# Cross-attention and feed-forward on one core: loads of CT and VQ and stores of VS issued by ScalarE, values taken one batch per step

## What is computed

```python
q = fq_sym((layernorm(x) @ Wq + bq) * scale, axis=-1)      # per row and head
k, v = split(cond @ Wkv + bkv)
k = fq_sym(k, axis=-1)
v = fq_sym(v, axis=2)                                       # one scale per column, over all keys
attn = fq_unsigned(softmax(q @ k.T), axis=-1)
x = x + (attn @ v) @ Wp + bp
xq = quant_input(layernorm(x)); x1, x3 = split(xq @ w13.T)
x = x + quant_input(rmsnorm(relu(x1)**2 * x3) * norm_w) @ w2.T
```

## Time and profile before

| | |
|---|---|
| Median of 3 runs | 1955.6 us |
| Profiled execution | 1956.41 us, its span 1954.5 us |
| TensorE | 85% busy, granted clock 0.90 of 2.4 GHz on average |
| VectorE | 87% busy |
| ScalarE | 70% busy |
| GpSimd | 74% busy |
| DMA queue of SyncE | packets take 80.3% of 16 engines' span, 325.38 MB |
| The loop's exps | from 186.6 to 1685.8 us |

### The profile page before, as it was taken

The page is one execution under the profiler, slowest core; times in us unless marked ns, Lnnn a source line. Parts: engine busy times, 40 slices in busy tenths (PEclk is TensorE's granted clock), DMA queues, the critical chain, the costliest instruction groups (busy, mean ns, idle before and its releaser), DMA issues.

```text
span 1954.5 us, 40604 instructions
## 1 busy us (share of the span) xinstructions
PE 1665.0 (85%) x16216; PEld 1134.0 (58%) x16216; DVE 1693.2 (87%) x2665; ACT 1372.1 (70%) x1324; POOL 1444.0 (74%) x1166
## 2 busy tenths in 40 slices
PE   7997888888788888887888888878988888579997
PEld 6884666665555666555566564434445555368875
DVE  6766999999879999997999999989999999776663
ACT  2445988898688888886888888777778778532221
POOL 1341788998898888988898899988997888623222
PEclk9998999998989999987999997556688998789999
DMA  5676989998989899999999998997988987642221
GB/s 166 220 204 164 197 192 196 181 202 183 211 167 205 181 199 184 188 199 195 193 189 186 203 177 167 198 165 135 184 161 157 207 168 144 129 111 45 63 55 44
DMA packets 862283, 327.97 MB, mean 168 GB/s; under 512 B 786128, under 2 KB 815888, under 8 KB 862096
## 3 DMA queue, kind: packets, MB, share of 16 engines
q1 hardware_dynamic: 862096, 325.38, 80.3%
HBM read 83.30 MB, written 48.63 MB: 67 GB/s over the span
## 4 chain that ended last, share of the span: by engine, by line
DVE 38%; PE 25%; issue 14%; POOL 11%; DMA 6%; ACT 5%; SPq 2%; POOLq 0%; DVEq 0%; ACTq 0%
DVE S L1141 34%; POOL PT L1384 7%; PE PS L660 5%; PE PS L764 5%; DMA PP<-Pr 3%; PE PK L815 3%; PE PK L600 3%; PE PS L627 2%; ACT Pr L967 2%; PE PK L602 2%; PE PO L679 2%; POOL VQ L1319 1%; PE PO L600 1%; PE PO L602 1%; SPq L544 1%
## 5 line engine op out<-in xcount | busy, mean ns | idle before, releaser
L1141 DVE TENSOR_SCALAR_CACHE_REDUCE S<-PS,SQN 128x1536 f32<-128x1536 f32 (+1 forms) x768 | 1287.0, 1714 | 92.0 <-PE PS L660 73.6
L967 ACT ACTIVATE Pr<-S,MS 128x5888 uint8<-128x5888 f32 x200 | 1041.4, 5207 | 234.7 <-DVE MJ L1163 157.2
L1384 POOL CAST PT<-PP 128x1536 uint16<-128x1536 uint8 (+1 forms) x800 | 1097.5, 1417 | 90.7 <-DMA PP<-Pr 89.3
L660 PE MATMUL PS<-KT,QT 96*128 96x512 bf16 (+1 forms) x2496 | 717.5, 413 | 132.8 <-DVE S L1141 121.6
L679 PEld LDWEIGHTS PO<-VI,PT 128*128 128x128 f16 x9200 | 349.4, 99 | 327.6 <-issue 144.1
L679 PE MATMUL PO<-VI,PT 128*128 128x32 bf16 x9200 | 365.9, 180 | 91.9 <-ACT AO L925 66.0
L660 PEld LDWEIGHTS PS<-KT,QT 96*128 96x128 bf16 (+1 forms) x2496 | 210.0, 105 | 343.1 <-issue 164.6
L600 PE MATMUL PK<-WG,CT 128*128 128x128 f32 (+1 forms) x1272 | 223.7, 306 | 14.1 <-DMA CT<-ctxt 9.5
L602 PE MATMUL PK<-CT,WG 128*128 128x128 f32 (+1 forms) x1272 | 212.0, 294 | 0.0
L600 PEld LDWEIGHTS PK<-WG,CT 128*128 128x128 f32 (+1 forms) x1272 | 175.6, 202 | 17.3 <-issue 13.2
L602 PEld LDWEIGHTS PK<-CT,WG 128*128 128x128 f32 x1272 | 166.3, 193 | 1.4
(11 more groups left out here) (154 smaller groups left out, 1456.0 us busy)
## 6 DMA issues: line engine op xcount, KB each, us to landing
CT<-ctxt SPq DMA_DIRECT2D x180, 256.0 KB, 3.3
k_rows<-KS SPq DMA_DIRECT2D x44, 512.0 KB, 4.1
v_rows<-VS SPq DMA_DIRECT2D x33, 256.0 KB, 4.0
VQ<-v_rows SPq DMA_DIRECT2D x33, 256.0 KB, 3.8
q_rows<-QS SPq DMA_DIRECT2D x13, 512.0 KB, 4.1
W13F<-w13T SPq DMA_DIRECT2D x16, 352.0 KB, 4.1
PP<-Pr SPq DMA_TRANSPOSE x200, 6.1
XT<-x SPq DMA_DIRECT2D x12, 256.0 KB, 3.3
```

What stands on the lines that cost most here:

```text
L660: last = pe.matmul(PS[n % 2][p0:p0 + r, f:f + w], QT[h % 3][0:PARTS * HD, q0:q0 + r], KT[h % 3][0:PARTS * HD, c * CHUNK + f:c * CHUNK + f ...
L967: act.activation(Pr[i % 2].rearrange("p t q b -> p t b q"), S[i % 2].rearrange("p (t b q) -> p t b q", b=2, q=P), ACT.Exp, bias=MS[:, i % ...
L1141: v.tensor_scalar(S[i % 2][:, c * CHUNK:c * CHUNK + CW[c]], PS[n % 2][:, 0:CW[c]], neg_step, None, ALU.mult, ALU.min, accum_out=MN[:, i % ...
L1384: gp.tensor_copy(PT[i % 2][:, 2 * t0:2 * t1, :].rearrange("p (t b) q -> p t b q", b=2), PP[i % 2][:, t0:t1, :].bitcast(U8).rearrange("p t ...
```

## The change

ScalarE gets `load_unit`, `store_v` and `load_v` and issues them in its step right behind exp(i); inside the loop SyncE no longer issues them (ahead of the loop it still loads CT). The waits ahead of each DMA are the same and move with it. The transposes stay on SyncE. The values are taken over twelve steps: one load of VQ per step, `v_quant` due at the last unit's step + 4.95 + b, and `turn_v`, which follows `v_loads`, one per step.

```diff
             for b in range(NBT):
-                v_loads.setdefault(STEP_OF_UNIT[g, NU - 1] + 4 + b // 2, []).append((g, b))
+                v_loads.setdefault(STEP_OF_UNIT[g, NU - 1] + 4 + b, []).append((g, b))
...
         @block.sync
...
                     if u == 0:
                         load_wg(g)
-                    load_unit(g, u)
-                for g, b in dve_batches.get(i, []):
-                    store_v(g, b)
                 for g, b in dve_batches.get(i - K_STORE, []):
                     store_k(g, b)
-                for g, b in v_loads.get(i, []):
-                    load_v(g, b)
...
         @block.scalar
...
+            def load_unit(g, u):
+                k = g * NU + u
+                n = unit_rows(u)
+                act.wait_ge(M["s_ku"], k - RING + 1)
+                act.dma_start(CT[k % RING][:, :, 0:n], ctxl if u == NU - 1 else ctxt[u]).then_inc(s_ct[k % RING], 16)
+
+            def store_v(g, b):
+                kb, us = g * NBT + b, BATCH[b]
+                act.wait_ge(M["s_kve"], g * NU + us[-1] + 1)
+                act.dma_start(Vd[g - 1, :, us[0] * P:(us[-1] + 1) * P],
+                              VS[kb % 2][:, 0:len(us) * P]).then_inc(M[f"s_vd{kb % 2}"], 16)
+
+            def load_v(g, b):
+                kb, us = g * NBT + b, BATCH[b]
+                act.wait_ge(M[f"s_vd{kb % 2}"], 16 * stored_v(kb))
+                if kb >= NBT + 3:
+                    act.wait_ge(M["s_vg"], kb - NBT - 2)
+                act.dma_start(VQ[kb % 3][:, 0:len(us) * P],
+                              Vd[g - 1, :, us[0] * P:(us[-1] + 1) * P]).then_inc(s_vq[kb % 3], 16)
...
                                scale=-1.0, accum_out=ZB[:, i:i + 1]).then_inc(M["s_exp"], 1)
+                for g, u in UNITS.get(i + 3, []):
+                    load_unit(g, u)
+                for g, b in dve_batches.get(i, []):
+                    store_v(g, b)
+                for g, b in v_loads.get(i, []):
+                    load_v(g, b)
                 for g, b in dve_batches.get(i - K_SPLIT, []):
                     k_high(g, b)
...
         @block.gpsimd
...
-                             (end + 4.95 + b // 2, v_quant, (g, b))]
+                             (end + 4.95 + b, v_quant, (g, b))]
```

More of the change, by code:

```diff
@@ L331, in load_unit @@
                 sp.dma_start(CT[k % RING][:, :, 0:n], ctxl if u == NU - 1 else ctxt[u]).then_inc(s_ct[k % RING], 16)
-            def store_v(g, b):
-                kb, us = g * NBT + b, BATCH[b]
-                sp.wait_ge(M["s_kve"], g * NU + us[-1] + 1)
-                sp.dma_start(Vd[g - 1, :, us[0] * P:(us[-1] + 1) * P],
-                             VS[kb % 2][:, 0:len(us) * P]).then_inc(M[f"s_vd{kb % 2}"], 16)
             def store_k(g, b):
@@ L355, in load_wg @@
                 sp.dma_start(WG[:, :, 1, :], wkv_v[:, :, C + g * GC:C + (g + 1) * GC]).then_inc(M["s_wg1"], 16)
-            def load_v(g, b):
-                kb, us = g * NBT + b, BATCH[b]
-                sp.wait_ge(M[f"s_vd{kb % 2}"], 16 * stored_v(kb))
-                if kb >= NBT + 3:
-                    sp.wait_ge(M["s_vg"], kb - NBT - 2)
-                sp.dma_start(VQ[kb % 3][:, 0:len(us) * P],
-                             Vd[g - 1, :, us[0] * P:(us[-1] + 1) * P]).then_inc(s_vq[kb % 3], 16)
             def turn_v(g, b):
```

## The result

After: 1980.28 us (median of 6 runs, 1972.48 to 1997.42), against 1960.07 us of the kernel before in the same runs (1954.83 to 1965.29): ratio 1.0115, interval [1.0083, 1.0148]. The forecast was 1937 us, faster. The kernel is 1.15% slower, and the time lies outside the predicted range of 1920 to 1978. The profiled execution took 1980.81 us, its span 1979.0, with a granted clock of 0.887 on average.

The account below looks back on a forecast made before the run. No engine is full; most of the loop runs at VectorE's pace, with 40.0 us lost to a ring where values are taken. 1956.4 - 40.0 + 14 + 0 + 5 + 2 = 1937.4, forecast 1937 us, range 1920 to 1978.

Parts of the forecast that it names:

- Two queues: DMA engines: PP, no longer in line with CT, may land later by what a CT takes; 5 us, bounds 0 and 15.
- The rule set against this step: DMAs of several engines share 16 DMA engines, only issue time is saved; read so that VQ lands no sooner, 1953.
- The value stretches: Three twelve-step stretches taking values of groups 1 to 3: 40.0 us lost, 14 to stay; some 94, 92 and 86 us.
- Exp's wait for PP: Sign of being right: exp's waits for the transpose of the probabilities under 35 us in all instead of 77.1.
- GpSimd was to wait under 8 us for VQ: Sign of being right: GpSimd's waits for the loads of VQ, 20.5 us before, under 8 us.
- the sign that bunching was not the cause: Sign of being wrong: the three stretches where values are taken stay over 97 us.
- The issues: Loads of CT, stores and loads, 105 us of issues, move to ScalarE's queue and lie under exp's 5.21 us; 0.
- The hold of ScalarE behind a PP issue: In the slower rival: one hold behind a 4.06 us PP issue in each of 36 store steps, up to 146 us.
- Later values: Group 1's last transposes of VB land 2.3 to 3.6 us late for TensorE once; some 2 us at VectorE.
- The rival that was slower: ScalarE pays for issues between exp and the next unit's evacuation: 36 us over 36 store steps, 1973; chance 0.17.
- the small terms: Terms beside the value stretches: issues 0, two queues 5, later values 2 us; their bounds give the likeliest case's range.
- The range: Likeliest case's own range 1922 to 1946 us; with the rivals 1920 to 1978, some 2 in 10 left out.

Follow-up runs that it names:

- all three with pairs: Changed kernel with the old schedule: loads of CT and VQ and stores of VS on ScalarE, values two batches per step; 1.0214 against the kernel before, 1998.03 us.
- the good version: Kernel before with values one batch per step and each load of VQ issued a step earlier, all DMAs on SyncE; 0.9878, 1934.91 us.
- the quarter loads: Kernel before with CT's loop loads issued by ScalarE, only 32 of 128 partitions loaded; 0.9940, against 0.9953 with the same cut loads on SyncE.

## Why the prediction was wrong

**"Two queues" is the step that failed.** It was put at 5 us, with bounds 0 and 15, because a PP "may land later by what a CT takes" and ScalarE had 0.9 us a step to spare. The runs give 20 us for the loads of CT, 21 us for the stores of VS and nothing clear for the loads of VQ; all three with pairs cost 2.1%. Two things were missed. First, how long a PP is delayed, and how many are: 108 of the 200 have an issue of ScalarE that starts inside their own, and land in 8.0 us instead of the 6.6 of the same steps before, the worst in 13.5. No row of the kernel before could give that, since it has no second issuer. Second, the slack was read off the wrong engine. ScalarE had room on average, but PP's ring runs over SyncE and GpSimd, which in the same neighbours had 78.4 of 88.9 and 76.2 of 87.0 us busy and a transpose to wait for. The page already showed exp waiting 77.1 us for PP, 34 times, and GpSimd 89.3 us: that was the tile whose landing to price.

The rule set against this step, that DMAs of several engines share 16 DMA engines and only issue time is saved (the Trainium skill, "DMA: Bandwidth & Descriptors", Issuing engines are not separate DMA queues), points the right way, and these runs go further: here the second issuer did harm. As predicted against that rule, VQ did come in time when issued from ScalarE (waits of 6.3 instead of 32.7 us at the same schedule), and a load placed one step earlier on SyncE did it at no cost.

**The value stretches: right in direction, too much by 8 us.** 26 of 40 us were to come back, 18.4 did. The stretches were to be 94, 92 and 86 us, which is 28 us less and not the sum's 26; they were 100.0, 97.7 and 84.2. With only the values' DMAs on ScalarE 22.8 came back, and 29 with the early loads on SyncE, so 11 left where 14 were taken. The 4.4 us between 22.8 and 18.4 go with the loads of CT, the one difference between those two kernels. Exp's wait for PP was to fall under 35 us. It rose to 99.7; in the good version it is 36.9. GpSimd was to wait under 8 us for VQ, and waited 17.0. Two of the three stretches stayed over 97 us, which was to be the sign that bunching was not the cause. As a sign it misleads: spreading together with early loading brings these two to 93.1 and 93.8.

**The issues: right.** They were put at 0, since ScalarE's queue runs ahead of exp. Of the 131 loads of CT, 102 start within 0.1 us of their exp, 23 up to 2 us ahead of it and none more than 0.5 us behind. They take 0.34 us in the median, and the quarter loads, as many, cost nothing that can be told apart. The cover's worth was shown as well: ahead of exp the same issues cost 20 us more. The hold of ScalarE behind a PP issue that was feared (146 us) did not come; with a PP issue of 6.38 us running, CT's took 0.36.

**Later values: low.** 2 us were taken for step 54; VectorE waits 4.6 us there in the kernel after and 7.3 in the good version. TensorE waits for the last VI there (3.9 and 6.2 us), as was argued.

**The rival that was slower** had the sign, and its 1973 us lay nearest to the 1980, by luck: its mechanism, ScalarE paying for the issues, was not the one. The harm done to a transpose by a copy from elsewhere was given as a small term of the forecast and not as a rival.

**The range.** Its lower end of 1922 is the sum with the small terms at their low bounds. With the same terms at their high bounds the sum is 1956.4 - 40.0 + 9 + 12 + 0 + 15 + 2 = 1954.4 and not 1946, so by its own bounds the forecast reached well into what can't be told from no change.

**In sum**, against before: the schedule -0.2%, the loads of CT +1.0% (priced with pairs), the stores of VS +1.1% (priced on the good version), and the loads of VQ on ScalarE -0.4% (22.8 instead of 15.2 us back in the value stretches, from one trace each). That makes +1.5%, where +1.15% was measured: the same within the intervals of the single prices, or the prices do not simply add.

**What stays open.** Whether it is the second queue or the moment of the issue is not told apart: from SyncE the same copies are issued in order with the transposes and never beside one that is still being issued. A run that could tell was not made: in the loop of the kernel before no transpose is in flight for 124.8 us in all, with 19 gaps of over 2 us, and none of the runs puts ScalarE's copies there. Part of the loss may come through TensorE's clock (0.89 against 0.94 in steps 52 to 88); no run held it fixed. Why the stores are dear only in steps 52 to 136 and not in the first forty (299.8 us with them on ScalarE, though 12 of the 36 are there), and the loads of CT hardly at all in 52 to 88, was not tried.

## What to carry to other kernels

Before moving DMAs to another engine's queue, find the transfer that the chain waits for and ask which copies will now be issued into it; here the price went with their bytes and with where they fell, not with the number of issues. A load that comes late can be issued one step earlier in the same queue, which cost nothing here. Spreading a burst and loading it early gave 1.2% together where neither alone gave anything clear, so try such a pair together before dropping its halves. Read the slack of a transfer off the ring that it closes, not off an engine that has time to spare. And where an issue is put behind a wait, the profile may name the issue for the whole of that wait.

## What the hardware showed that was not expected

- With everything on one queue, the 200 DMA transposes of the loop land in 6.1 us in the median and 9.8 at most. With direct copies of 256 KB from a second queue the median is 7.1 and the longest 13.5. Most of the delay falls on the transposes that are being issued when a copy goes out: 1.3 us on average with a whole load of CT (91 transposes), 0.9 with half and 0.5 with a quarter, against the same steps with all on SyncE. Copies that SyncE issued itself were beside a transpose just as long (94 and 95% of the flight of a CT).
- The DMA engines' busy share does not say how fast bytes go: queue shares add up to 127.6% at 288 GB/s and to 123.7% at 143 GB/s.
- ScalarE's queue issues a DMA while an ACTIVATE of 5.21 us is running, in 0.34 us in the median of the loads of CT. An issue placed behind that instruction's wait but ahead of it delays it by its own length and a little more, 0.38 us from the issue's start to exp's.
- A transpose being issued by SyncE for 4 to 6 us did not hold up an issue of ScalarE (0.36 us beside one of 6.38); the longest of the 36 loads of VQ took 2.55 us to issue. PP's own issue did not grow either: 4.2 us on average for the 108 with an issue of ScalarE inside, and 4.2 for the same steps of the kernel before.
